# A graph convolution and mixture-of-experts kernel: two accumulators for the neighbour maximum, and another order of pairs and products on TensorE

## The reference

```python
def _graph_conv_max(x, src, dst, W_rel, b, W_root):
    agg = jax.ops.segment_max(x[src], dst, num_segments=N)
    agg = jnp.where(jnp.isfinite(agg), agg, 0.0)
    return agg @ W_rel.T + b + x @ W_root.T
...
h = relu(_graph_conv_max(layernorm(x), src, dst, W1_rel, b1, W1_root))
h = relu(_graph_conv_max(h, src, dst, W2_rel, b2, W2_root))
x = x + h
...
probs = softmax(layernorm(x) @ Wr, axis=0)          # over the nodes
vals, idx = top_k(probs.T, 512)                     # per expert
x = x + scatter_add(vals * (gelu(sel @ W1 + b1) @ W2 + b2))
```

## Time and profile before

| what | value |
|---|---|
| runs | 1024.95, 1025.27 and 1028.95 us, median 1025.27 |
| span of the profiled execution, its first to its last instruction | 1025.1 us |
| PE busy | 726.0 us (71%), 2541 matmuls |
| DVE busy | 681.6 us (66%), 1232 instructions |
| ScalarE busy | 270.3 us (26%) |
| GpSimd busy | 546.7 us (53%), 372 gathers among it |

### The profile page before, as it was taken

The page is one execution under the profiler, slowest core; times in us unless marked ns, Lnnn a source line. Parts: engine busy times, 40 slices in busy tenths (PEclk is TensorE's granted clock), DMA queues, the critical chain, the costliest instruction groups (busy, mean ns, idle before and its releaser), DMA issues.

```text
span 1025.1 us, 9702 instructions
## 1 busy us (share of the span) xinstructions
PE 726.0 (71%) x2541; PEld 329.5 (32%) x2541; DVE 681.6 (66%) x1232; ACT 270.3 (26%) x389; POOL 546.7 (53%) x537
## 2 busy tenths in 40 slices
PE   0317555778378778866488657887698678789996
PEld 0214222333133323322133323333243235344442
DVE  3768565588758767873888774898588879733120
ACT  0264250222022202222434030343243122012222
POOL 5652326557746675764556655566447200565644
PEclk9757877899789989987899878998899889899999
DMA  5715336557746675656657756666566400377656
GB/s 136 219 36 183 101 97 184 162 170 214 216 116 194 184 218 144 202 168 184 174 177 214 226 163 180 189 213 193 158 193 187 143 12 1 113 235 142 105 102 82
DMA packets 64770, 162.18 MB, mean 158 GB/s; under 512 B 16383, under 2 KB 20755, under 8 KB 64709
## 3 DMA queue, kind: packets, MB, share of 16 engines
q0 software_dynamic: 40448, 124.74, 44.6%
q1 hardware_dynamic: 17004, 17.16, 6.0%
q10 hardware_dynamic: 7272, 19.74, 5.9%
HBM read 143.37 MB, written 18.11 MB: 158 GB/s over the span
## 4 chain that ended last, share of the span: by engine, by line
PE 33%; DVE 25%; issue 19%; another core or an unknown queue 9%; ACT 5%; POOL 3%; DMA 2%; DVEq 2%; POOLq 0%; ACTq 0%; SPq 0%
PE pp L1165 8%; DVE acc L891 6%; PE prow L1136 5%; PE pp L1563 5%; DVE weights L902 5%; PE pp L1576 4%; PE prow L1103 3%; PE prow L1124 2%; DVE mem L1403 2%; POOL mem L838 1%; DMA mem<-tab,ic 1%; PE pp L1346 1%; PE prow L519 1%; PE pp L501 1%
## 5 line engine op out<-in xcount | busy, mean ns | idle before, releaser
L838 POOL DMA_INDIRECT mem<-tab,ic x372 | 389.5, 1047 | 266.9 <-issue 136.5
L1165 PE MATMUL pp<-weights,slots 128*128 128x512 bf16 x1200 | 306.8, 405 | 114.8 <-DVE acc L891 70.2
L891 DVE TENSOR_TENSOR acc<-acc,pp 128x1024 f32<-128x1024 f32 x180 | 219.1, 1217 | 85.3 <-PE pp L1165 33.5
L1165 PEld LDWEIGHTS pp<-weights,slots 128*128 128x128 bf16 x1200 | 118.0, 103 | 307.5 <-issue 103.8
L902 DVE TENSOR_TENSOR weights<-weights,mem 128x1024 f32<-128x1024 f32 x129 | 158.1, 1226 | 17.9 <-DVE weights L902 11.3
L1136 PE MATMUL prow<-weights,aggT 128*128 128x512 f32 x160 | 92.2, 708 | 37.4 <-ACT aggT L1213 20.5
L1124 PE MATMUL prow<-weights,rootT 128*128 128x512 f32 x160 | 76.0, 619 | 0.0
L1615 POOL DMA_INDIRECT out<-mem,node_of x28 | 44.2, 1577 | 47.3 <-ACT mem L1593 40.9
L1544 DVE COPY weights<-prow 128x512 f32<-128x512 f32 x28 | 18.7, 688 | 72.1 <-PE prow L1103 71.7
L1604 POOL DMA_INDIRECT mem<-xnd,slot_of x20 | 22.0, 1099 | 78.4 <-DVE weight_of L1538 72.6
L1213 ACT ACTIVATE aggT<-prow 128x512 f32<-128x512 f32 x20 | 11.9, 597 | 192.5 <-PE prow L1103 98.7
(11 more groups left out here) (349 smaller groups left out, 828.0 us busy)
## 6 DMA issues: line engine op xcount, KB each, us to landing
slots<-ttd ACTq DMA_DIRECT2D x20, 640.0 KB
mem<-tab,ic POOLq DMA_INDIRECT x372
weights<-in_L_ffn_W SPq DMA_DIRECT2D x9, 512.0 KB, 5.1
weights<-in_L_ffn_W ACTq DMA_DIRECT2D x7, 512.0 KB
xnd<-xin ACTq DMA_DIRECT2D x10, 256.0 KB
mem<-in_x SPq DMA_DIRECT2D x2, 1120.0 KB
tab<-mem SPq DMA_DIRECT2D x1, 2240.0 KB
weights<-in_L_gnn_W_rel SPq DMA_DIRECT2D x2, 1024.0 KB
```

What stands on the lines that cost most here:

```text
L838: g.indirect_dma_start(ring[:, h * PAIR + k, :], None, tables[l], bass.IndirectOffsetOnAxis(ic[:, j * PAIR + k:j * PAIR + k + 1], 0))\
L891: v.tensor_tensor(acc[:, :, :], acc[:, :, :], pp[j % 2][:, :, :], ALU.max).then_inc(S["pa"], 1)
L1165: ins = t.matmul(pp[j % 2][:, i, :], sel[u][:, j * KP + i, :], hot[:, j, w, :], start=w == 0, stop=w == 2)
```

## The change

A second accumulator is laid over three old tensors (`spare`), and the tiles use `acc` and `spare` in turn, so that the wait for the aggregate (`fin`) at the start of a tile goes. The register loads of a tile's bounds (`extent`) are made ahead of the merge of the tile before. A tile starts with the maximum of gathered pairs 0 and 1 (`first_two`); the join takes gathered pair 2 (`pe_first`), and gathered pair 3 follows PE's pair 1 (`pool_after_first`). The loop begins at gathered pair 4 and the one that stood behind pair 7 is in it. In layer 2, the add moves behind pair 3 and the guess behind pair 4. On PE pair 2 stands ahead of the aggregate's product, whose second half stands between pairs 3 and 4, and the root product is split around pair 6.

```diff
-        hst, x2t = sb("hst", [P, D]), sb("x2t", [P, D])
-        xnT = sb("xnT", [P, C, P])
+        spare = sb("spare", [P, 3 * D])
...
+        accs = [acc[:, :, :], spare[:, 0:2 * D].rearrange("p (a d) -> p a d", a=2)]
...
-            def first_three(k, lo):
...
+            def first_two(k, lo):
+
+                if k % NQ == HEAVY:
+                    v.wait_ge(S["ready"], first_pair + lo + (FLYING + 1))
+                    v.scalar_tensor_tensor(accg, carry[:, :].unsqueeze(1).to_broadcast([P, 2, D]), cap[:, :],
+                                           in_ring(lo), ALU.min, ALU.max).then_inc(S["done"], 1)
+                else:
+                    v.wait_ge(S["ready"], first_pair + lo + (FLYING + 2))
+                    v.tensor_tensor(accg, in_ring(lo), in_ring(lo + 1), ALU.max).then_inc(S["done"], 2)
+
+            def pe_first(k, lo):
+
+                slot = lo + 1 if k % NQ == HEAVY else lo + 2
+                v.wait_ge(S["ready"], first_pair + slot + (FLYING + 1))
+                v.wait_ge(S["pairs"], k * PAIRS + 1)
+                v.tensor_tensor(accs[k % 2], in_ring(slot), pp[0][:, :, :], ALU.max).then_inc(S["pa"], 1)
+
+            def pool_after_first(k, lo):
+
+                slot = lo + 2 if k % NQ == HEAVY else lo + 3
+                v.wait_ge(S["ready"], first_pair + slot + (FLYING + 1))
+                v.wait_ge(S["done"], first_pair + slot + (SUBS - 1))
+                v.tensor_tensor(accg, accg, in_ring(slot), ALU.max).then_inc(S["done"], 2)
...
-                if k:
-                    v.wait_ge(S["fin"], k)
-                    v.sem_inc(S["apart_v"], 1)
...
-                    first_three(k, lo)
+                    first_two(k, lo)
+                    pe_first(k, lo)
                     pe_pair(k, 1)
+                    pool_after_first(k, lo)
                     pe_pair(k, 2)
+                    if q == HEAVY:
+                        pool_pair(lo + 3)
+                    pe_pair(k, 3)
                     if l:
                         add_and_moments(q - 1)
-                        pe_pair(k, 3)
+                        pe_pair(k, 4)
                         guess(q - 1)
...
                     pe_pair(k, 5)
-                    with v.Fori(3, m) as i:
+                    with v.Fori(4, m + 1) as i:
                         pool_pair(lo + i)
                     pe_pair(k, 6)
                     pe_pair(k, 7)
-                    pool_pair(lo + m)
                     pe_pair(k, 8)
                     pool_pair(lo + m + 1)
                     pe_pair(k, 9)
+                ahead = extent(q + 1) if q + 1 < NQ else None
...
                 if q:
                     neighbours(k - 1)
-                    neighbours_product(k - 1, (0, 1))
                 pairs(k, (2,))
                 if q:
+                    neighbours_product(k - 1, (0, 1))
+                pairs(k, (3,))
+                if q:
                     neighbours_product(k - 1, (2, 3))
-                pairs(k, (3, 4))
+                pairs(k, (4,))
...
-                    root_product(k, range(C))
-                pairs(k, (6, 7, 8, 9))
+                    root_product(k, (0, 1))
+                pairs(k, (6,))
+                if k != NQ:
+                    root_product(k, (2, 3))
+                pairs(k, (7, 8, 9))
```

More of the change, by code:

```diff
@@ L887, in pe_pair @@
             def pe_pair(k, j):
+                m = accs[k % 2]
                 v.wait_ge(S["pairs"], k * PAIRS + (j + 1))
                 v.wait_ge(S["pa"], k * PAIRS + j)
-                v.tensor_tensor(acc[:, :, :], acc[:, :, :], pp[j % 2][:, :, :], ALU.max).then_inc(S["pa"], 1)
+                v.tensor_tensor(m, m, pp[j % 2][:, :, :], ALU.max).then_inc(S["pa"], 1)
             def in_ring(slot):
@@ L974, in merge @@
                 v.sem_inc(S["apart_v"], 1)
+                m = accs[k % 2]
                 if l:
-                    v.scalar_tensor_tensor(acc[:, :, :], accg, BIG, acc[:, :, :], ALU.min, ALU.max).then_inc(S["merge"], 1)
+                    v.scalar_tensor_tensor(m, accg, BIG, m, ALU.min, ALU.max).then_inc(S["merge"], 1)
                 else:
-                    v.tensor_tensor(acc[:, :, :], acc[:, :, :], accg, ALU.max).then_inc(S["merge"], 1)
+                    v.tensor_tensor(m, m, accg, ALU.max).then_inc(S["merge"], 1)
                 v.wait_ge(S["merge"], NQ + 2 * q + 1 if l else q + 1)
@@ L982, in merge @@
                 if l == 0:
-                    v.tensor_tensor(agg[:, :], acc[:, 0, :], acc[:, 1, :], ALU.max).then_inc(S["fin"], 1)
+                    v.tensor_tensor(agg[:, :], m[:, 0, :], m[:, 1, :], ALU.max).then_inc(S["fin"], 1)
                     if q == 0:
@@ L1037, in vec_tile @@
                 else:
-                    first_three(k, lo)
+                    first_two(k, lo)
+                    pe_first(k, lo)
                     pe_pair(k, 1)
+                    pool_after_first(k, lo)
                     pe_pair(k, 2)
+                    if q == HEAVY:
+                        pool_pair(lo + 3)
+                    pe_pair(k, 3)
                     if l:
                         add_and_moments(q - 1)
-                        pe_pair(k, 3)
+                        pe_pair(k, 4)
                         guess(q - 1)
                     else:
-                        pe_pair(k, 3)
-                    pe_pair(k, 4)
-                    if l == 0 and q:
-                        clamp(q - 1)
+                        pe_pair(k, 4)
+                        if q:
+                            clamp(q - 1)
                     pe_pair(k, 5)
-                    with v.Fori(3, m) as i:
+                    with v.Fori(4, m + 1) as i:
                         pool_pair(lo + i)
@@ L1061, in vec_tile @@
                 merge(k)
+                return ahead
             if l:
@@ L1075, in build @@
                 v.wait_ge(S["xin"], 16 * NQ)
+            bounds = extent(0)
             for q in range(NQ):
-                vec_tile(l * NQ + q)
+                bounds = vec_tile(l * NQ + q, *bounds)
             if l == 0:
```

35 lines of the change are left out of this document (12 added, 23 removed).

## The result

| | before | changed |
|---|---|---|
| median, us | 1025.11 (1017.04 to 1028.95, 4 runs) | 1049.55 (1044.54 to 1056.95, 4 runs) |
| ratio | | 1.0259, 95% interval 1.0191 to 1.0326 |
| profiled execution, span | 1025.1 | 1049.9 (its time 1052.02) |
| granted clock over the span | 0.884 | 0.875 |
| TensorE idle before the selector matmuls | 114.8 | 154.0 |

The change costs 24 us, 2.6%. The prediction, 1021.5 with a range of 1007 to 1038, was wrong in its sign, and the result lies above the range. Rival A (1036) named the right mechanism but not enough of it.

A forecast was written before the change was run, and what follows sets the result against it. Neither TensorE (71% busy) nor VectorE (66%) was full; they hand work to and fro through two PSUM pairs. The terms summed as 1025.1 + 1.1 + 5 - 4 - 5.7 = 1021.5 us, range 1007 to 1038.

The forecast's parts named there:

- Rival A: Layer tile starts on PE: the clock falls at every one, slower, 1036 us; chance 0.25.
- Step 1: DVE's start of undisturbed tiles: gathered maximum at about +0.62, join at +1.76 us, moved register load costing nothing.
- rival C: Tile starts: the change only moves waits, the join needing three landed gathered pairs instead of one; 1025 us, chance 0.12.
- Step 2: PE's pair 2 ahead of the product in undisturbed tiles: +0.1 us a tile, eleven tiles, +1.1 us.
- Step 3: Root product in two halves around pair 6: costs and gains nothing in an undisturbed tile.
- Step 4: TensorE's clock at tile starts: pause 2.9 us, 1.76 a fall, half of six layer 1 starts, +5 us.
- Step 5: Gathers in the heavy tiles of both layers: POOL's earlier lead covers the loop's waits, -4 us.
- Step 6: Disturbed tiles, with late PE results: waits stay, but the moved maximum lies inside them in about five tiles, -5.7 us.

The follow-up runs named there:

- i1: The kernel before with DVE's part alone (second accumulator, new lead, moved register load, layer 2's add and guess later), PE's order and root product unchanged: 949.99 us, ratio 1.0053.
- h3: The changed kernel, unaltered, run again on chip 5 against the kernel before: 960.97 us, ratio 1.0179.
- h4: The changed kernel with seven matmuls of 384 columns a tile added on PE, results unread: 952.81 us, ratio 1.0084 to the kernel before.
- i2: The kernel before with only PE's order changed, pair 2 ahead of the aggregate's product: 971.86 us, ratio 1.0292.
- e5: The changed kernel with the root product in one piece before pair 6 again, on chip 2: ratio 1.0152 to the kernel before.
- g4: The kernel before with only the root product split in two halves around pair 6, on chip 4: ratio 1.0001.
- f2: The kernel before with the new lead, one accumulator, and layer 2's add and guess one pair later, on chip 3: ratio 1.0238.
- g1: The kernel before with half the bytes in every gather, half the ring zero-filled first, on chip 4: 948.53 us, ratio 1.0041.
- h1: The kernel before with half the bytes in every gather, half the ring zero-filled first, on chip 5: 947.50 us, ratio 1.0038.
- f4: The changed kernel with the register load of the bounds back at its tile's start, on chip 3: ratio 1.0132 to the kernel before.
- f3: The changed kernel, unaltered, run again on chip 3: ratio 1.0257 to the kernel before.

## Why the prediction was wrong

**Step 1** was right to a few hundredths where it could be seen: maximum at +0.61, join at +1.74, 1.13 behind it. The rule that the prediction took from the Trainium skill, VectorE: DVE Perf Modes, section "The DRAIN you can't avoid", is that an operation starts only when the pipe is empty; the same section adds that one which is not held starts earlier, which the prediction left out. The join starts 1.13 us behind a maximum that takes 1.22, so here it was not held back, and the measurement decides. What step 1 gave in time is i1's tile, 25.7 us for 26.48. The step failed in one thing: it let the join's need of a third landed gather cost nothing. That was rival C's "for", and it is the 2.29 us at tile 4 of h3, where PE has only pair 2 to go on with and that needs the join; in i1, where the product stands first, 1.51 us of the same wait cost nothing.

**Step 2** was right in its distances: pair 2 at +3.01, and where the clock held (h4), pair 4 at +10.5 for +10.7 and the tile at 26.54 for 26.6 (26.48 and 0.1). The add behind pair 3 was also right, as i2 shows by its absence.

**Step 3** was right for the kernel before, 1.0001. In the changed kernel it is not tested: e5, without the halves, had 1.0152 on chip 2, and the changed kernel 1.0259 and 1.0257 on chips 1 and 3.

**Step 4** failed, and it is the main failure. The pause of 2.9 us was exact, the price of 1.76 also (1.7 by the tiles 5 and 8 of h3 and h4). The count of falls was not. I gave half of six layer 1 starts a fall and layer 2 none. In h3 six starts fell that had not in g4, the tiles 4, 5, 6 and 8 and, in layer 2, 11 and 12; on chip 1 sixteen starts were slow, eight more than before, four of them in each layer, which is 14 us instead of 5. The pause of most layer 2 tiles had hardly grown where nothing else was late (2.48 to 2.71 us in h3, 2.35 to 2.40 in g4), and I held that against a fall. But a start that had just escaped had no margin: in the trace of before a pause of 2.4 us was followed by a fall at 655 and by none at 544, and one of 2.7 by a fall at 516, a row that the prediction passed over. One pause grew by construction. In tile 11, the first of layer 2, a copy for the heavy tile (`carry`) follows the aggregate, the gathered maximum stands behind it, and PE's pair 2 starts at +4.03: 2.70 us became 4.64, in h3 as on chip 1, with a fall in both. And I took each pause as the undisturbed one, where on chip 1 five more of layer 2's were 4.4 to 6.3 us long. That throttled is the default and activity lifts it (the Trainium skill, TensorE: Matmul & The Clock Gate, Part 1) fits what the fillers did: work whose result nobody reads made the tile 1.7 us shorter.

**Step 5**, -4, failed. The loop of the heavy tile waits for landed gathers, 5.7 us in 5 waits in g4 and 5.1 us in 4 in h3. Both heavy tiles together took 75.3 us in g4 and 75.4 in h3. DVE's loop eats a pair every 1.42 us, and POOL issues a pair's two gathers in 2.5, so an earlier start did not last to the loop's end. In i1 and h4, with the same lead, the two tiles took 78.6 and 78.0. The same lead made the tile behind layer 2's heavy one 2.9 us shorter (29.21 to 26.32) and the one behind layer 1's 4.3 longer (25.14 to 29.44, of it 2.29 the join's wait and 1.8 a fall).

**Step 6**, -5.7, was of the right size for the tiles it spoke of: on chip 1 the tiles 4, 13, 14 and 17 came down by 2.6, 1.5, 0.6 and 1.5, together 6.2. But I had let the late results stay where they were. They did not: tile 1 got 2.1 longer, and the undisturbed tiles took part in them.

In sum, on a chip without late results the forecast's own terms, without 5 and 6, would have been +6; 17.6 came. Of these the six falls are 10.6 and the join's wait at tile 4 is 2.3; the other 4.7 are not split. On chip 1 24.4 came for -3.8. Of the 28 between, 9 are falls (14 for 5) and 4 are step 5; the other 15 lie with the late results, and what these gave and took is not split either. The range failed because it took falls and late results as alternatives (1036 was the worst case of the one, with the gains of steps 5 and 6 still deducted), where both got worse together.

## What to carry to other kernels

Here an order that puts a dependent pair first left PE without work in the wait, and the falls of its clock cost more than the order gave. Price the longest pause that a new order makes, and count every pause that stands near one with a fall as one that can fall too. A wait that moves from behind PE's work to in front of it costs its length (2.29 us at tile 4), and the same kind of wait behind PE's work cost none (1.51 us in i1); ask of each new lead how many landed transfers it needs where the transfers are behind. And put the kernel before beside every experiment on its own chip: here the chip changed the time by four times what the change did, and the order of the variants with it.

## What the runs showed of the hardware

- The same kernel took 1025, 1045 and 1049 us on three chips and 944, 943 and 944 on three others. Its runs spread from 1033 to 1059 on chips 2 and 3, and over 6.4 us or less on each of the chips 4 to 6. Part of the difference shows as results of PE that DVE and ACT take 2.5 to 10.8 us after the matmul's row ends (331.94 to 334.49 in f2, 275.04 to 285.88 in the earlier trace rows); its cause is open.
- Seven matmuls of 384 columns a tile, whose results nothing reads, made the changed kernel 8.2 us faster (960.97 to 952.81).
- Gathers of 1 KB rows instead of 2 KB took 6.5 and 3.7 us off the stretch from the first to the last aggregate (575.4 in g1 and 578.3 in h1 for the 582.0 of g4), about 1%, though they halve the bytes. The whole kernel was no faster, 948.53 and 947.50 us for 944.41 and 943.36, since the fill of the ring comes before.
- With two gathered pairs in flight instead of three the changed kernel took 1.046 of before (chip 4), with three 1.018 (chip 5).
- A register load of 0.3 us behind a running maximum costs DVE nothing (the next operation 1.36 us behind, with or without it); in front of the first one of a tile it put PE's pair 2 0.54 us later (+3.56 in f4 for +3.02 in f3).
